# One program for three stages: the experts' opening laid into the last causal batch, weights ahead of residual rows, the last batch routed ahead

## The reference

```python
x = x + tanh(g_xattn) * cross_attention(layernorm(x), ctx)      # 16 heads of 32, relative bias
y = layernorm(x)
y = y + causal_attention(rmsnorm(y))                            # 16 heads, latent keys, rotary part
n = rmsnorm(y)
shared  = (silu(n @ sWg) * (n @ sWu)) @ sWd                     # one shared expert, width 256
probs   = softmax(n @ Wgate + expert_bias)                      # 8 experts, the best 2, renormalised
routed  = sum over the 2 chosen experts e of p_e * ((silu(n @ Wg[e]) * (n @ Wu[e])) @ Wd[e])
x = x + tanh(g_ffn) * (y + shared + routed)
```

## Time and profile before

| | us |
|---|---|
| median of 3 runs | 2329.98 (2328.88 to 2330.65) |
| the profiled execution, its own time | 2325.74 |
| its span, first to last instruction | 2324.0 |
| busy in it: PE, DVE, POOL, ACT | 2103.3, 1489.1, 1374.2, 1180.0 |

### The profile page before, as it was taken

One profiled execution on the slowest core, in us unless ns is written; L12 is line 12 of the kernel. 1 busy time (PEld: TensorE's weight loads), 2 busy tenths in 40 slices (PEclk: granted clock), 3 DMA queues, 4 the chain that ended last, 5 costly groups with the idle time before them and its releaser, 6 DMA issues. The chain is left out here.

```text
span 2324.0 us, 43302 instructions
## 1 busy us (share of the span) xinstructions
PE 2103.3 (91%) x12568; PEld 958.9 (41%) x12569; DVE 1489.1 (64%) x4180; ACT 1180.0 (51%) x2319; POOL 1374.2 (59%) x1450
## 2 busy tenths in 40 slices
PE   2899999999999977799999999999984897899997
PEld 1333333333333312344444444544432443455554
DVE  3688888888888874466566565655544678344443
ACT  3355555555555544345545455554544673455554
POOL 4267776776776765255656565665661575455554
PEclk7999999999999987899999999999997998999999
DMA  5513323232332222534535354353514676666665
GB/s 161 168 55 110 101 85 103 81 115 73 107 97 92 78 98 86 170 115 139 159 118 153 117 163 134 114 174 98 155 49 159 120 156 126 114 116 112 115 109 91
DMA packets 227973, 272.15 MB, mean 117 GB/s; under 512 B 40152, under 2 KB 165964, under 8 KB 227508
## 3 DMA queue, kind: packets, MB, share of 16 engines
q1 hardware_dynamic: 197324, 212.76, 30.3%
q0 software_dynamic: 22752, 47.86, 12.1%
q10 hardware_dynamic: 7704, 9.20, 1.2%
HBM read 161.82 MB, written 86.54 MB: 107 GB/s over the span
## 5 line engine op out<-in xcount | busy, mean ns | idle before, releaser
L501 ACT ACTIVATE a_pt<-a_bank 128x512 f32<-128x512 f32 x512 | 305.6, 597 | 370.2 <-DVE a_bank L608 367.3
L1439 DVE CUSTOM_DVE_ANT_0 b_bank<-b_bank,b_tri 128x256 f32<-128x256 f32 (+3 forms) x512 | 253.2, 497 | 296.0 <-PE b_bank L1579 291.8
L619 DVE CUSTOM_DVE_ANT_0 a_bank<-a_bank,a_strip 128x512 f32<-128x512 f32 x512 | 353.2, 691 | 4.6 <-PE a_bank L762 3.9
L1192 POOL TENSOR_TENSOR b_acc<-b_acc,b_pt 128x256 f32<-128x256 f32 (+2 forms) x384 | 279.2, 749 | 84.2 <-ACT b_pt L1305 73.3
L411 POOL TENSOR_TENSOR a_acc<-a_acc,a_pt 128x512 f32<-128x512 f32 x256 | 317.5, 1271 | 16.2 <-ACT a_pt L501 15.7
L608 DVE TENSOR_TENSOR a_bank<-a_bank,a_band 128x256 f32<-128x256 f32 (+1 forms) x512 | 205.6, 402 | 129.7 <-PE a_bank L749 128.5
L1305 ACT ACTIVATE b_pt<-b_bank 128x256 f32<-128x256 f32 (+2 forms) x384 | 143.7, 383 | 187.1 <-PE b_bank L1563 171.1
L749 PE MATMUL a_bank<-a_q_stack,a_k_stack 128*128 128x512 f16 x512 | 199.2, 390 | 22.9 <-ACT a_pt L501 13.9
L762 PE MATMUL a_bank<-a_k_stack,a_q_stack 97*128 97x512 f16 x512 | 196.4, 384 | 3.6 <-DVE a_low L619 3.5
L1964 POOL DMA_INDIRECT out_dram<-c_z,c_to_row x71 | 112.5, 1585 | 133.8 <-DMA out_dram<-c_z,c_to_row 97.6
L1578 PE MATMUL b_bank<-b_k_stack,b_q_stack 96*128 96x256 f16 (+3 forms) x512 | 154.6, 302 | 16.0 <-DVE b_low L1439 8.7
(11 more groups left out here) (338 smaller groups left out, 5352.7 us busy)
## 6 DMA issues: line engine op xcount, KB each, us to landing
b_q_stack<-qk_rows SPq DMA_DIRECT2D x192, 128.0 KB, 2.6
a_q_stack<-qk_rows SPq DMA_DIRECT2D x96, 128.0 KB
a_k_stack<-qk_rows SPq DMA_DIRECT2D x96, 128.0 KB
b_k_stack<-qk_rows SPq DMA_DIRECT2D x96, 128.0 KB, 2.6
a_sums<-in_x SPq DMA_DIRECT2D x34, 256.0 KB, 3.2
qk_rows<-a_qk_hi SPq DMA_DIRECT2D x64, 128.0 KB, 1.7
qk_rows<-a_qk_lo SPq DMA_DIRECT2D x64, 128.0 KB, 1.8
out_dram<-a_sums SPq DMA_DIRECT2D x32, 256.0 KB, 2.0
```

Of the source, the lines that this page charges most:

```text
L501: nc.scalar.activation(pt[:, n % SLOTS, :], st_bank[n % 2][:], ACT.Exp).then_inc(exped, 1)
L619: nc.vector.tensor_tensor_reduce(out=max_bank[step % 2][:], in0=max_bank[step % 2][:], in1=strip[:, g * HG + hh, at:at + S], scale=-1.0, s ...
L1192: nc.gpsimd.tensor_tensor(sums_of, sums_of, probs(n), ALU.add).then_inc(pooled, 1)
L1439: nc.vector.tensor_tensor_reduce(out=max_bank[step % 2][:, 0:w], in0=max_bank[step % 2][:, 0:w], in1=tri[:, at:at + w], scale=-1.0, scalar ...
```

## The change

The experts' stage becomes a third generator, and `run_all` joins it to the second: from step 38 of the body "last" of `pass_b` on, each engine takes one step of the third stage after each step of the second. The third stage's opening has OPENING = 90 such steps; in each engine its work is laid out over them. Behind the opening every engine waits for the last output row of the attention (`all_used`). The tiles of the third stage are ordered anew in memory, so that those of the opening lie where the second stage's tiles have been read for the last time; the shared expert has tiles of its own (`own_gu_hi` and so on), the banks are numbered anew, and the identity is the second stage's.

```diff
+NEXT_JOIN = 38
+OPENING = 2 * UNITS - NEXT_JOIN
             def body(kind, b, u):                                   # pass_b, SP
...
+                if kind == "last":
+                    yield
                 if kind in ("steady", "last", "end"):
                     for t in range(NT):
                         sp.wait_ge(left_dve, upto(kind, b, (O, t), by_dve))
...
             def body(kind, b, u):                                   # pass_b, POOL
+                if kind == "steady" and b == 2:
+                    pool.wait_ge(past_first, 4)
+                    for s in first_pass.used:
+                        pool.sem_clear(s)
+                    pool.sem_inc(first_cleared, 1)
...
             yield from over(body)
-            for s in first_pass.used:
-                pool.sem_clear(s)
+        def inputs_used(eng):
+            eng.wait_ge(first_cleared, 1)
+            eng.wait_ge(summed, (B - 1) * (UNITS // HG))
+            eng.wait_ge(stacked[G3], B * STK)
+        def all_used(eng):
+            eng.wait_ge(left_dve, upto("end", B, (O, NT - 1), by_dve))
```

SP's opening (all its loads but `z` 2 and 3, behind the stacks of the last batch and ahead of the stores of batch 6), and its loop, in which the weights now come before the rows:

```diff
+            prior.inputs_used(sp)
...
             up_weights(0)
             down_weights(0)
             load_z(1)
+            sp.dma_start(table, blank_rows).then_inc(blanked, 16)
+            yield
+            prior.all_used(sp)
             load_z(2)
+            sp.wait_ge(prior.z1_stored, 64 * B + 16)
+            sp.nop(nofuse=True)
             load_z(3)
             for b in range(B):
+                up_weights(b + 1)
+                down_weights(b + 1)
...
                 if b and b + 3 < B:
                     load_z(b + 3)
-                up_weights(b + 1)
-                down_weights(b + 1)
```

```diff
+            for s in range(OPENING):
+                if s == 13:
+                    prior.inputs_used(pe)
...
+                    pe.wait_ge(prior.lowered, B * UNITS)
+                if 13 <= s < 13 + NT:
+                    turn(0, s - 13)
+                if s == 40:
+                    pe.wait_ge(prior.vacated, B * NG)
+                    pe.wait_ge(const_loaded, 16 * 10)
+                    pe.wait_ge(r_split, NK)
+                    route(0)
+                    pe.wait_ge(prior.exped, B * UNITS)
+                    pe.wait_ge(w_split, PARTS)
+                    up(0, 0, 0)
+                yield
+            prior.all_used(pe)
```

In the batches both casts of expert b + 1 are in batch b (`up_weights` in its middle on ScalarE and VectorE, `down_weights` behind `hidden_high(b, 1)`), and batch 7 is routed a piece earlier (`early` is b == 6):

```diff
             for b in range(B):                                      # DVE
+                more, early = b + 1 < B, b + 2 == B
                 if more:
+                    settle(b)                                       # shares, read_ranks, place_rows
...
                 else:
                     lay_starts()
+                    lay_blocks()
                 activate(b, 0)
...
+                up_weights(b + 1)
+                if early:
+                    choose(b + 1)
                 activate(b, 1)
+                if early:
+                    settle(b + 1)
+                elif more:
+                    choose(b + 1)
+                else:
+                    low_part(1)
+                    set_from_row(Count(0, 0, 4))
+                    set_from_row(Count(0, 1, 4))
+                    set_from_row(Count(0, 2, 4))
+                down_weights(b + 1)
                 for t in range(NT):
                     finish_rows(b, t)
```

TensorE does `route(7)` between `up(6, 1, 0)` and `up(6, 1, 1)` and `rank(7)` between the halves of `down` of batch 6, and `x_turn` of block 0 before it waits for the weights and for `out_done`. GpSimd:

```diff
-                for _ in range(min(n, left[0] - (B - 1 - b) * NT)):
+                known = B if b >= B - 2 else b + 1
+                for _ in range(min(n, left[0] - (B - known) * NT)):
...
             pool.wait_ge(out_stored[2], 32)
-            for j in range(3):
+            for j in range(4):
                 gather(Count(0, j, 4))
             add_to_output(B - 1)
-            for i in range(4):
-                pool.wait_ge(out_stored[i], 16 * (B // 4))
             def step(at):
-                if not at.within(NB - 3, NB):
+                if not (at.within(0, 0) or at.within(NB - 3, NB)):
                     gather(at.back(-3))
+                if at.within(2, 2):
+                    for i in range(4):
+                        pool.wait_ge(out_stored[i], 16 * (B // 4))
```

432 lines of the change are left out of this document (250 added, 182 removed).

## The result

The changed kernel takes 2297.89 us (median of 4 runs, 2296.36 to 2299.8), the kernel before 2329.43 beside it (4 runs, 2320.46 to 2330.65). The ratio is 0.9872, 95% interval 0.9853 to 0.9892: 1.3% faster. The forecast was 2286, with 2274 to 2303 as range: the time lies inside the range and 12 us above the forecast. The profiled execution took 2299.8 us, its span is 2297.9; before they were 2325.74 and 2324.0.

A forecast was written before the change was run, and what follows sets the result against it. PE was taken as the bound, idle mainly in two late holes and two long batches. Terms −31.7 +9 +1.5 +0 −11 +2.5 −14 = −43.7 took 2325.7 to 2282.0; plus 4.2 for the median, 2286 us, range 2274 to 2303.

The forecast's parts named there:

- The opening: Between the attention's last row and batch 0's first share: 32.0 us removed, less some 0.3 for the rank product, −31.7.
- +9: Attention's last steps: the interleaved work delays them, ScalarE 6.9, GpSimd 1, TensorE 2, taken as 9 us; bounds 6 and 14.
- +1.5: Attention's last steps: early loads, late small copies and semaphore clearing together cost 1.5 us; bounds 0 and 5.
- a rival, at 4.4 in all: Attention's last sums: VectorE's casts stop GpSimd through the shared ports, +4.4 us, 2290 us in all; chance 0.05.
- Batch 0: First expert batch: clock gives back 1 to 3 us, ScalarE waits some 3 for loads; 0, from −3 to +4.
- −11: Expert batches after the first: ScalarE's stall for weights goes, since loads are released earlier; −11 us, bounds −2 and −15.
- +2.5: Batches 6 and 7: routing the last batch early puts VectorE work ahead of PE's; +2.5 us, bounds 0 and 5.
- the DMAs keep the long batches: Rival for the long expert batches: transfers keep them long, at most −2 gained, expert 1's load costs 4; 2299 us, chance 0.12.
- The gap: Between the last batch and the blocks: earlier table and gathers cut 28.7 us to 10.0 + 4.5, −14; bounds −17 and −7.
- The likeliest case: Whole kernel: the forecast itself, 2279 to 2294 us, chance 0.57.
- three conditions under which I had called the prediction wrong: Attention's end slips over 15 us, ScalarE waits in mid-batch for weights, or block 0 still waits for its gather.
- the rivals at 2297 to 2299: Attention's last steps cost 20 us, 2297, chance 0.12; or transfers keep the long expert batches, 2299, chance 0.12.

The follow-up runs named there:

- the opening behind: Changed kernel with the opening's computation joined to the attention at step 85 instead of 38, loads left where the change put them: 2294.85 us, ratio 0.9841.
- the low parts: Changed kernel with VectorE's casts for the shared expert's weights in steps 15 to 18 instead of 19 to 23: 2300.14 us, ratio 0.9867.
- the weights ahead: Changed kernel with expert 1's weight transfers issued by the sync engine before its waits for the last residual rows: 2294.47 us, ratio 0.9841.
- the choice moved: Changed kernel with shared-expert casts earlier, expert 1's transfers earlier, and batch 6's choice of batch 7 behind its hidden rows: 2293.38 us, ratio 0.9828.

## Why the prediction was right, and where it wasn't

*The opening, −31.7 for −32.0.* Right in size. But the reason given, that its work would be issued ahead of 1756.1, was only half needed: the run with the opening behind shows that 16.7 us go without work laid between the units' steps.

*The attention's end, +9 and +1.5 for +15.3.* The +1.5 fits, though 1.2 us is within this stretch's spread: with the computation away and the loads kept, the end came 1.2 us later, with PE's wait of 1.48 for row maxima as its new stall. The +9 is the term that was mis-sized, 14.1 in its place (63.8 less 49.7), and the mechanism behind it was wrong. I packed ScalarE's work, 6.9 us too much of it. ScalarE is indeed busy 23.06 of 26.55 us up to 1738, but taking twelve passes out of that stretch gave 0.8 us, and nothing once the low parts had moved. Of the 14.1 the runs showed 3.4 to be VectorE and GpSimd holding each other up; I had priced that as a rival, at 4.4 in all. For the rest no kernel was run, but the traces say on which engine it lies. The windows from S to the last row: before, in the changed kernel, with the opening behind; then the changed kernel's operations on the experts' banks alone:

```profile
1707.59:1756.11 48.52, 38.43 (x279) 15.88 (x271) 13.83 (x39) 19.09 (x45) 26.43 (x36) 0.96 0.05 18
1709.43:1773.26 63.83, 50.05 (x355) 21.84 (x347) 27.88 (x71) 37.14 (x89) 32.14 (x53) 0.84 0.20 73
1706.13:1755.81 49.68, 40.30 (x286) 16.84 (x279) 14.05 (x42) 24.31 (x62) 28.27 (x51) 0.93 0.25 93
1709.43:1773.26 63.83, 6.91 (x76) 4.35 (x76) 2.96 (x5) 2.45 (x4) 0.84 0.20 73
```

Of the 15.3 us 11.6 are PE's busy time and 3.7 its idle time; against the opening behind, of 14.1, 9.8 and 4.4. The opening's 76 products take 6.91 us, and the attention's own 279 take 44.33 for 38.43 (the two overlap by some 1.2). The granted clock is 0.84 in place of 0.96; by that alone I estimate 38.43 × 0.96 / 0.84 = 43.9 us for them. I had put TensorE's part at 2: of its 8.96 us I counted only the products of `route(0)` and `up(0, 0, 0)`, not the transposes ahead of them, and nothing for a lower clock on the attention's products. That is the step that failed here. What made the clock fall is open.

*Batch 0, 0 for +6.8,* outside the bounds of −3 and +4. The failed step: ScalarE "waits for three loads of 6.9 us that overlap: some 3 us". It waited 11.66 us, because the sync engine's own wait for the last rows stands ahead of the loads, which go out at 1775.45 to 1778.13, 2 to 5 us behind the last row. The gate and up weights go out from 1776.43 on, and the cast starts at 1786.95. The clock gave nothing back: it is 0.78 in batch 0, and 0.86 in the same batch with the weights ahead.

*Batches 1 to 7, −11 and +2.5 for −2.4.* Also mis-sized, and the −11 the more so, as the changed kernel's trace has the shortest batches 1 to 5 of all that share its code there: batch 4's stall went (24.7 to 19.3 us), batch 2's only shrank (28.0 to 25.5). ScalarE's wait for weights was a stall in front of another, GpSimd's queue. I had GpSimd busy 15.65 us in the window of 19.3 and 19.51 in that of 28.0 in front of me, and didn't add the idle 0.30 us ahead of most scatters that this leaves out. The rival "the DMAs keep the long batches" had the right time and the wrong engine. Routing ahead cost batch 6 some 4.3 us (I had 1.5), and gave them back as a wait saved.

*The gap, −14 for −14.9.* Right, and the runs split it. Over batch 7 and the gap together, 15.3 us, they show 9.0 for the outputs' wait moved behind the gathers and 5.8 for the blocks laid early. The routing ahead, which I named first, only gives back there what it costs in batch 6 (4.4 and 4.3 us); with it the parts come to more than the whole, so they overlap.

The likeliest case, 2279 to 2294, didn't hold: two of the three conditions under which I had called the prediction wrong came true, ScalarE's wait in mid-batch, and the attention's end over 15 us late. The range held since it reached to the rivals at 2297 to 2299, of which parts of two occurred together: that is the width of the range, not the forecast's mechanism.

## What to carry to other kernels

When a serial opening is to be hidden, first move its loads, and measure; computation laid between the steps of a stage whose TensorE is busy 0.86 of the time already (24.47 of 28.35 us) can cost about what it saves (14.1 us here, for 15.3). Count every product that moves, also the transposes, and look at the clock of those that were there. When a stall is removed, add up the queue of the engine that is next: an engine with 18 us of issue in a period of 19 is the next stall, and moving its work only moves the place. And ask of each load which wait stands ahead of it on the issuing engine.

## What was unexpected in the hardware

*Two engines, both slowed.* From 1739.89 to 1748.06 VectorE did five casts and GpSimd a product, three sums and a low part. Apart, these take 2.73 + 1.22 and 5.34 us, 9.3 in all; beside each other they took 8.2, most of the way to one running after the other. I had counted a loss for GpSimd only; VectorE lost 3.3 us, GpSimd 2.6. The Trainium skill, page "SBUF — State Buffer", section "SBUF: two separate sides", says that whichever of the two starts first holds the shared ports for the whole instruction and the other waits, in either direction. The trace agrees in that both lose, with 5.21 us for casts of 2.73 and 4.26 for sums of 2.91.

*A small copy behind large ones.* ScalarE's copy of the row maxima, 4 KB, lands 5.2 us after its issue (3.0 for the same copy before) when the opening's loads are in flight; a 256 KB store takes 8.2 (2.0). In variants the copy took up to 6.7. The DMA rows of the changed kernel, 1700 to 1725 (count, KB each, median us to landing):

```profile
z_all<-b_sums SPq DMA_DIRECT2D x4, 256.0 KB, 8.2
...
b_q_stack<-b_m_row ACTq DMA_DIRECT2D x1, 4.0 KB, 5.2
```

Left open: why that same copy makes PE wait 1.5 us in one variant and 3.1 in another; why the stretch behind it takes 9.6 us in three of the traces and 11.3 in most others; why batches 1 to 5 take 104.6 to 110.0 with the same code; and why at S, up to which the runs compute the same, the traces lie 9 us apart. A join between steps 38 and 85 was not tried, nor the opening behind together with the low parts or the choice moved. The changed kernel was not timed again beside the variants, so that their times compare with its own only through the ratios.
